# Attention 1: a loop of its own, with split context as weights of the values product and the division on GpSimd

## The reference

```python
def _L1_xattn_ref(x, context, Wq, Wk, Wv, Wo, bo):
    HEADS = 16
    DIM_HEAD = 64
    SCALE = DIM_HEAD ** (-0.5)
    ...
    q = (x @ Wq).reshape(B, N, HEADS, DIM_HEAD).transpose(0, 2, 1, 3)
    k = (context @ Wk).reshape(B, M, HEADS, DIM_HEAD).transpose(0, 2, 1, 3)
    v = (context @ Wv).reshape(B, M, HEADS, DIM_HEAD).transpose(0, 2, 1, 3)
    dots = jnp.einsum('bhnd,bhmd->bhnm', q, k) * SCALE
    attn = jax.nn.softmax(dots, axis=-1)
    out = jnp.einsum('bhnm,bhmd->bhnd', attn, v)
    out = out.transpose(0, 2, 1, 3).reshape(B, N, HEADS * DIM_HEAD)
    return out @ Wo + bo
```

## Time and profile before

| what | us |
|---|---|
| median of 3 executions | 4946.03 |
| the profiled execution | 4941.79 |
| its span | 4940.1 |
| of that, attention 1's rounds, first scores to the next stage's first matmul | 1349.3 to 2873.7 |

### The profile page before, as it was taken

How to read it: one execution, slowest core, us unless ns; L and a number is a source line. 1 busy time by engine, 2 the same in 40 slices (tenths; PEclk the granted TensorE clock), 3 DMA queues, 4 the chain that set the end, 5 groups by cost and what they waited for, 6 DMA issues and landing times. The chain is left out here.

```text
span 4940.1 us, 100893 instructions
## 1 busy us (share of the span) xinstructions
PE 4273.6 (87%) x34007; PEld 3601.8 (73%) x34007; DVE 3320.7 (67%) x6505; ACT 2358.4 (48%) x5328; POOL 1276.1 (26%) x1182
## 2 busy tenths in 40 slices
PE   5399999994599999999999968788699999959684
PEld 4277777773499999999999955566577777747573
DVE  4477777765566666666666677887677777755545
ACT  0056666662144444444444446666366666634341
POOL 0122222221201101111010036676222222214320
PEclk6589999996799999999999988898799999979796
DMA  7344545430100100010010010000445454410371
GB/s 239 104 102 110 110 99 117 104 74 10 43 20 25 30 25 25 20 34 23 22 35 20 11 35 18 18 0 1 90 110 111 100 118 105 103 45 1 86 184 39
DMA packets 102723, 316.97 MB, mean 64 GB/s; under 512 B 36391, under 2 KB 44889, under 8 KB 102425
## 3 DMA queue, kind: packets, MB, share of 16 engines
q1 hardware_dynamic: 98840, 294.71, 25.5%
q10 hardware_dynamic: 3584, 18.43, 1.0%
HBM read 146.07 MB, written 19.54 MB: 34 GB/s over the span
## 5 line engine op out<-in xcount | busy, mean ns | idle before, releaser
L1394 ACT ACTIVATE a1m_prob<-a1m_ps_s,a1m_neg_max 128x500 f32<-128x500 f32 x672 | 447.3, 674 | 585.4 <-DVE a1m_neg_max L1318 585.4
L1237 PE MATMUL a1m_ps_o<-a1m_cn,a1m_prob_t 125*128 125x96 f32 x5376 | 633.2, 274 | 0.4 <-issue 0.4
L1237 PEld LDWEIGHTS a1m_ps_o<-a1m_cn,a1m_prob_t 125*128 125x128 f32 x5376 | 619.8, 192 | 0.6 <-issue 0.6
L1315 DVE TENSOR_REDUCE a1m_bank_max<-a1m_ps_s 128x1 f32<-128x500 f32 x672 | 455.7, 678 | 214.5 <-PE a1m_ps_s L1203 212.6
L729 DVE TENSOR_REDUCE a0m_bank_max<-a0m_ps_s 112x1 f32<-112x500 f32 x768 | 489.0, 669 | 153.4 <-PE a0m_ps_s L593 148.7
L729 DVE TENSOR_REDUCE a2m_bank_max<-a2m_ps_s 112x1 f32<-112x500 f32 x768 | 488.9, 669 | 149.3 <-PE a2m_ps_s L593 144.8
L1203 PE MATMUL a1m_ps_s<-a1m_cxt,a1m_qhi 98*128 98x500 f32 x1344 | 442.9, 411 | 19.8 <-issue 13.1
L812 ACT ACTIVATE a0m_prob_t<-a0m_ring 125x448 f32<-125x448 f32 x768 | 391.3, 545 | 96.7 <-PE a0m_ring L547 92.8
L812 ACT ACTIVATE a2m_prob_t<-a2m_ring 125x448 f32<-125x448 f32 x768 | 391.2, 545 | 94.7 <-PE a2m_ring L547 90.9
L1165 POOL TENSOR_TENSOR a1m_cxt<-a1m_raw,g_zeros 98x1500 fp32r<-98x1500 f32 x32 | 86.6, 2707 | 1281.9 <-PE a1m_ps_s L1203 1234.1
L1219 PE MATMUL a1m_ps_t<-g_ident,a1m_prob 128*125 128x128 f32 x2688 | 377.7, 277 | 0.4 <-ACT a1m_prob_t L1402 0.3
(11 more groups left out here) (778 smaller groups left out, 9251.7 us busy)
## 6 DMA issues: line engine op xcount, KB each, us to landing
a0m_ks<-a0m_k_hi SPq DMA_DIRECT2D x256, 187.5 KB
a2m_ks<-a2m_k_hi SPq DMA_DIRECT2D x256, 187.5 KB
a0m_ks<-a0m_k_lo SPq DMA_DIRECT2D x128, 187.5 KB
a2m_ks<-a2m_k_lo SPq DMA_DIRECT2D x128, 187.5 KB
ctx_t<-cprep_tr ACTq DMA_DIRECT2D x32, 562.5 KB
a0m_raw<-ctx_t SPq DMA_DIRECT2D x32, 562.5 KB
a1m_raw<-ctx_t SPq DMA_DIRECT2D x32, 562.5 KB
a2m_raw<-ctx_t SPq DMA_DIRECT2D x32, 562.5 KB
```

What stands on the lines that cost most here:

```text
L1237: m = pe.matmul(ps_o[at, 0:C], prob_t[:, u % 2, t, at], cn[:, h, t, :], start=(t == 0), stop=(t == KT - 1))
L1315: dve.tensor_reduce(bank_max[:, s, k:k + 1], ps_s[:, k, 0:BK], AX.X, ALU.max).then_inc(bank_maxed, 1)
L1394: act.activation(prob[:, s, k * BK:(k + 1) * BK], ps_s[:, k, 0:BK], ACT.Exp, bias=neg_max[:, s:s + 1], accum_out=bank_den[:, s, k:k + 1]). ...
```

## The change

Attention 1 gets its own function, `attend_heads`; `attention` keeps the case of attention 3. In it:

- The probabilities are divided before they are turned: GpSimd multiplies each bank (128x500) by the reciprocal of the denominator, in place (`divide`). `normalise`, `o_turn` and its copy go.
- The turned probabilities are split into float32r parts: ACT copies the high part of each bank from PSUM (`high_part`), DVE subtracts it from PSUM and writes the low part (`low_part`). Each bank of PSUM for the turned probabilities is used once per unit (three banks, `ps_t`), where there were two in turn.
- The context for the values product is split too, by GpSimd, and is now the weights (96 columns), with the turned probabilities of two or three units as the moving side (256 or 384 columns), in three products of parts for each of the twelve tiles. The result comes out turned.
- The products of a group of units are spread over steps by the table `pieces`; the four queries stand in steps 5, 7 and 10, project in step 3.
- PE's step is scores of u, project or one query, turn of u - 1, sums, a further query. DVE's is maxima of u, low part of u - 2, denominator of u, queries. ACT's is exps of u, the copy of a finished group, high part of u - 1. GpSimd's is the division of u and one piece of the context's split. The clears at the stage's start go, and the queries' bias, which is zero here.
- The three `pick` tables of `constants` go; where they were read (twice each, on ACT), `pick` writes the same from columns of `g.ident`.

```diff
             pool.memset(g.hm64[:], 1.0).then_inc(cleared, 1)
-            picks = ((g.pick_f0, 12, 64), (g.pick_f1, ME, 128), (g.pick_f2, 8, 256))
-            for tile, _, _ in picks:
-                pool.memset(tile[:], 1.0).then_inc(cleared, 1)
...
-            for tile, cols, width in picks:
-                v = tile[:].rearrange("e (c w) -> e c w", w=width)
-                pool.affine_select(out=v, in_=v, compare_op=ALU.is_equal, fill=0.0, base=0,
-                                   pattern=[[-1, cols], [0, width]], channel_multiplier=1).then_inc(cleared, 1)
...
+def attend_heads(nc, g, name, ctx_d, ctx_t, ob, a_w, vo):
...
+    nu, heads, hq, nq, width = 2 * HEADS * L // P, HEADS, TC // PAIR, HEADS // (TC // PAIR), HEADS * L
+    su, total, R = nu // 2, nu * NP, 4
+    members = ((0, 1), (2, 3), (4, 5, 6))
+    place = (0, 1, 2, 3, 0, 1, 2, 3, 2, 0, 1, 2, 3, 1)
+    free_at = (-1, 0, 0, 0, 1, 1, 2, 2, 3, 3, 3, 4, 4, 5)
+    pieces = {4: (0, 0, 0, 0, 6, False), 5: (0, 0, 0, 6, 12, False), 6: (0, 0, 1, 0, 6, False),
+              7: (0, 0, 1, 6, 12, False), 8: (0, 0, 2, 0, 4, True), 9: (0, 0, 2, 4, 12, False),
+              11: (0, 1, 0, 0, 6, False), 12: (0, 1, 0, 6, 12, False), 13: (0, 1, 1, 0, 6, False),
+              0: (-1, 1, 1, 6, 12, False), 1: (-1, 1, 2, 0, 4, True), 2: (-1, 1, 2, 4, 12, False)}
+    ask_at = {5: (0,), 7: (1,), 10: (2, 3)}
...
+        prob = st.sb("prob", [P, 2, S])
+        prob_t = st.sb("prob_t", [NK, 2, KT, R, P], F32R)
...
+        def rounds(eng, step):
+            for u in range(nu):
+                step(0, u, 0)
+            with eng.Fori(0, NP // 2 - 1) as j:
+                for b in range(2):
+                    for u in range(nu):
+                        step(2 * j + b + 1, u, 1 - b)
+            for u in range(nu):
+                step(NP - 1, u, 1)
+            for u in range(4):
+                step(NP, u, 0)
...
+            load_keys(0, 0)
+            load_vals(0)
+            load_keys(1, 1)
+            sp.wait_ge(vals_low, 3)
+            load_vals(1)
+            with sp.Fori(1, NP) as i:
+                for b in range(2):
+                    n = 2 * i + b
+                    sp.wait_ge(scored, BANKS * su * (n - 1))
+                    load_keys(n, b)
+                    sp.wait_ge(vals_low, 3 * n)
+                    load_vals(n)
...
+            def split(whole, high, low, made, done, count):
+                pool.tensor_tensor(high, whole, g.zeros[0:rows, 0:1].broadcast_to([rows, wide]), ALU.add
+                                   ).then_inc(made, 1)
+                pool.wait_ge(made, count)
+                pool.tensor_tensor(low, whole, high.bitcast(F32), ALU.subtract).then_inc(done, 1)
...
+            def divide(i, u):
+                v, s = nu * i + u, u % 2
+                pool.wait_ge(denned, v + 1)
+                for k in range(BANKS):
+                    at = slice(k * BK, (k + 1) * BK)
+                    pool.tensor_tensor(prob[:, s, at], prob[:, s, at], den[:, s:s + 1].broadcast_to([P, BK]), ALU.mult
+                                       ).then_inc(divided, 1)
+            def step(i, u, b):
+                h, s = u // su, u % su
+                if live(i, u, 0):
+                    divide(i, u)
+                n, j, o = 2 * i + h + 1, i + h, 1 - h
+                if s in (2, 3, 4) and among(n, 2 * NP):
+                    split_keys(n, j, o, s - 2)
+                if s in (5, 6) and among(n, 2 * NP):
+                    split_vals(n, o, s - 5)
+                if s == 0 and up(n - 1) and among(n - 1, 2 * NP):
+                    split_vals(n - 1, h, 2)
...
+                    pe.wait_ge(q_kept, nq * (i + 1))
+                rows = slice(u % su * P, (u % su + 1) * P)
+                for k in range(BANKS):
+                    if up(v):
+                        pe.wait_ge(exped, BANKS * (v - 1) + k + 1)
+                    keys = slice(k * BK, (k + 1) * BK)
+                    for n, (part, w) in enumerate(((qhi, 0), (qhi, 1), (qlo, 0))):
+                        m = pe.matmul(ps_s[:, k, 0:BK], part[:, b, h, rows], cxt[:, h, w, keys], start=(n == 0),
+                                      stop=(n == 2))
...
+            def turn(i, u):
+                v = nu * i + u
+                for k in range(BANKS):
+                    pe.wait_ge(divided, BANKS * v + k + 1)
+                    if up(v):
+                        pe.wait_ge(low, BANKS * (v - 1) + k + 1)
+                    for q in range(GT):
+                        t = k * GT + q
+                        m = pe.transpose(ps_t[k][0:NK, q * P:(q + 1) * P], prob[:, u % 2, t * NK:(t + 1) * NK],
+                                         g.ident[:])
+                    m.then_inc(turned, 1)
+            def sums(i, h, x, first, last):
...
+                    if t == first or t % GT == 0:
+                        pe.wait_ge(low, BANKS * end + t // GT + 1)
+                    for q, (w, p) in enumerate(((0, 0), (0, 1), (1, 0))):
+                        m = pe.matmul(out, cn[:, h, w, t * C:(t + 1) * C], prob_t[:, p, t, at:at + len(units), :],
+                                      start=(t == 0 and q == 0), stop=(t == KT - 1 and q == 2))
+                if last == KT:
+                    m.then_inc(summed, 1)
...
+            def step(i, u, b):
+                d, h, x, first, last, behind = pieces.get(u, (0, 0, 0, 0, 0, None))
+                ready = behind is not None and among(i + d, NP)
+                if live(i, u, 0):
+                    scores(i, u, b)
+                if u == 3 and among(i - 1, NP):
+                    project(i - 1)
+                asks = ask_at.get(u, ()) if live(i, u, 0) else ()
+                for q in asks[:1]:
+                    queries(i + 1, q)
+                if live(i, u, 1):
+                    turn(*((i, u - 1) if u > 0 else (i - 1, nu - 1)))
+                if ready and not behind:
+                    sums(i + d, h, x, first, last)
+                for q in asks[1:]:
+                    queries(i + 1, q)
+                if ready and behind:
+                    sums(i + d, h, x, first, last)
...
+            def queries(i, b, q):
+                src = ps_q[0:C, 0:hq * PAIR].rearrange("p (h b l) -> p b h l", h=hq, b=2)
...
+                dve.wait_ge(q_made, n + 1)
+                dve.tensor_copy(hi, src).then_inc(q_high, 1)
+                dve.wait_ge(q_high, n + 1)
+                dve.tensor_tensor(lo, src, hi.bitcast(F32), ALU.subtract).then_inc(q_kept, 1)
...
+            def low_part(i, u):
+                v = nu * i + u
+                for k in range(BANKS):
+                    tiles = slice(k * GT, (k + 1) * GT)
+                    dve.wait_ge(high, BANKS * v + k + 1)
+                    dve.tensor_tensor(prob_t[:, 1, tiles, place[u], :],
+                                      ps_t[k][0:NK, :].rearrange("p (t r) -> p t r", t=GT),
+                                      prob_t[:, 0, tiles, place[u], :].bitcast(F32), ALU.subtract).then_inc(low, 1)
+            def denominator(i, u):
+                v, s = nu * i + u, u % 2
+                dve.wait_ge(exped, BANKS * (v + 1))
+                if up(v - 1):
+                    dve.wait_ge(divided, BANKS * (v - 1))
+                dve.tensor_reduce(den[:, s:s + 1], bank_den[:, s, :], AX.X, ALU.add).then_inc(added, 1)
+                dve.wait_ge(added, v + 1)
+                dve.reciprocal(den[:, s:s + 1], den[:, s:s + 1]).then_inc(denned, 1)
+            def step(i, u, b):
+                if live(i, u, 0):
+                    maxima(i, u)
+                if live(i, u, 2):
+                    low_part(*((i, u - 2) if u > 1 else (i - 1, nu + u - 2)))
+                if live(i, u, 0):
+                    denominator(i, u)
+                    for q in ask_at.get(u, ()):
+                        queries(i + 1, 1 - b, q)
...
+            def high_part(i, u):
+                v = nu * i + u
+                done = 6 * i + free_at[u]
+                if up(done):
+                    act.wait_ge(summed, done)
+                for k in range(BANKS):
+                    act.wait_ge(turned, BANKS * v + k + 1)
+                    act.activation(prob_t[:, 0, k * GT:(k + 1) * GT, place[u], :],
+                                   ps_t[k][0:NK, :].rearrange("p (t r) -> p t r", t=GT), ACT.Copy).then_inc(high, 1)
...
+            def step(i, u, b):
+                if live(i, u, 0):
+                    exps(i, u)
+                d, h, x, _, last, _ = pieces.get(u, (0, 0, 0, 0, 0, None))
+                if last == KT and among(i + d, NP):
+                    keep_sums(i + d, h, x)
+                if u == 3 and among(i - 1, NP):
+                    out(i - 1)
+                if live(i, u, 1):
+                    high_part(*((i, u - 1) if u > 0 else (i - 1, nu - 1)))
...
-        full = heads == HEADS
-        gp = 1 if full else 2
+        if heads == HEADS:
+            attend_heads(nc, g, name, ctx_d, ctx_t, ob, a_w, vo)
+            return
...
```

(68 more changed lines are left out.)

237 lines of the change are left out of this document (177 added, 60 removed).

## The result

The changed kernel takes 5335.5 us (median of 4 runs, 5328.6 to 5348.4) where the kernel before takes 4947.5 (4 runs, 4934.3 to 4950.6): 1.079 times the time, with a 95% interval of 1.076 to 1.081. The forecast was 5346 us. Against the execution on which the sum was made, 4941.8, the profiled one of after (5331.3) has +389.5; forecast +404.

The account below looks back on a forecast made before the run. Attention 1 was taken as bound by PE's list. Profiled 4941.8 us, +302 for the added wait, +125 for the clock, -16 for the stage's start, -6.6 for the tables gave 5346 us, range 5200 to 5510.

Parts of the forecast that it names:

- The added wait: Attention 1: PE's turn waits for DVE's low part behind the maxima; rounds 111.7 us against 92.9, +302 us in all.
- The clock: Attention 1: PE's new 1.6 us gaps, in ten steps of fourteen, let the clock fall; 7.8 us a round, +125 us.
- half of them: Share of a round's ten PE gaps assumed to lose 1.56 us each to low clock: 5 x 1.56 = 7.8 us.
- rival 1: PE's gaps in attention 1 cost no clock: rounds of 111.7 us, 5221 us in all; chance 0.18.
- The products: Values product on PE: 0.123 us per 256 columns, 0.178 per 384; 30.5 us a round against 37.1.
- What is covered: Attention 1: work of ACT, GpSimd and SP's loads fits within the longer steps; GpSimd 5.5 to 6.5 us, under 7.7.
- that meeting: DVE subtraction while GpSimd runs, once seen at 3.64 us instead of 0.62; costed at nothing in the new loop.
- The rest: Outside the rounds: clears at the stage's start gone, -16 us; tables gone, -6.6 us; fill and drain 0.
- rival 2: Every gap in attention 1 drops the clock, a slow spell reaching the next gap: 5711 us; chance 0.11.
- Rival 3: PE does not stand in attention 1, if banks were freed before the maxima: rounds of 85.7, 4804 us; chance 0.07.
- Rival 4: GpSimd's division or split slower than any row, over 7.7 us a step: 112 us on top; chance 0.04.

Follow-up runs that it names:

- e1: The changed kernel with fourteen spare transposes on PE before the turn, in the ten steps with a gap and neither project nor query: 5203.7 us.
- e2: The changed kernel with five spare transposes on PE before the turn, in the ten steps with a gap and neither project nor query: 5210.4 us.
- e5: The changed kernel with two spare transposes on PE before the turn, in the ten steps with a gap and neither project nor query: 5240.9 us.
- e3: The changed kernel with only PE's order altered, the products of a finished group standing between scores and turn: 4959.4 us.
- e7: The changed kernel with products before the turn and the queries moved from steps 5, 7, 10, 10 to 1, 8, 10, 12: 4870.2 us, 0.985 times the kernel before.
- e6: The changed kernel with a spare fourth 128x500 operation on GpSimd before each unit's division: 5349.9 us.
- e8: The changed kernel with products before the turn, queries moved to steps 1, 8, 10, 12, and a spare 128x500 GpSimd operation before each division: 4870.2 us.
- e4: The changed kernel with only DVE's order altered, the low part of u - 2 before the maxima of u: 5097.8 us.

## Why the prediction was right, point by point

- **The added wait** was the core, and it holds in place, size and number: in most steps the turn starts 3.84 to 3.86 after the first score (3.87 forecast), and ordinary steps take 7.66 (7.7). e1 isolates the round without spells: 111.2 against 111.7. Step 3 was costed a little high, 6.84 (7.1). Step 10 takes 7.8 (8.2), but its last 0.4, the late second copy that holds the next maxima back, is there: it falls in step 11, whose turn starts at 4.24 and which takes 8.05.
- **The clock**: 1.56 us a spell, five a round, 7.8 a round. The spell's length was taken from one gap in the earlier trace rows, of three that cost 3.06, 1.56 and nothing, and "half of them" lay between bounds and was a choice, not a reading: that both hit to a tenth is luck. e1, e2 and e5 show that the spells hang on PE's idle time; why one gap of 1.65 us has one and the next has not stays open. The rule under "HAM oscillation — how this bites in real kernels" in the Trainium skill (TensorE: Matmul & The Clock Gate) would have left these gaps free of cost, and with it rival 1 would hold; the trace contradicts it with half of the gaps of 1.65 us.
- **The products**: from the first start to the next instruction, 18 products of 256 columns take 2.19 us in the rows at 3234.03 and 2.12 in e3's at 2616.22, so 0.118 to 0.122 each (0.123), and 24 of 384 take 4.19 in e7, so 0.175 (0.178). That is 11 to 15 ns above the columns at 2.4 GHz, where I took 17: a round's products take 29.6 to 30.2 us, forecast 30.5. By the 2.5 ns of the Trainium skill (the same page, "Wait — 56ns, not 53.3ns?") the estimate would be 27.4; the rows here lie nearer to the forecast, so leaving that rule out of the sum was right. The prediction called both rows evidence against it. Only the first is: 0.21 us for two products. The second row's 0.39 us is a length and not a distance between starts.
- **What is covered**: DVE and GpSimd are busy 53% and 54% of a stretch, a little under the 60% expected. The division took 1.02 us a bank (1.1), the split of 500 columns 1.02 and 1.25 (2.2 for both), and e6 adds another microsecond a step for nothing. The low part is 0.68 each (0.69), with GpSimd busy over half of the time, so costing that meeting at nothing was right. At steps of 6.3 us on average (88.2 / 14) the slack is nearly used up: the microsecond of e8 costs some 0.4 us a round. So the sentence "if steps were shorter, GpSimd would be the cover that fails" was a little too gloomy for PE's order; e4 shows when it does fail, when the maxima come late.
- **The rest**: start -17.3 (-16), tables -6.8 (-6.6). Some 5 us more came from untouched stages ahead of attention 1, for which no step of the prediction stands.
- **The rivals**: rival 1 is refuted by the clock of 0.92 and by e1; rival 2 by the spells' number. Rival 3 was out at once, since the order is as read; what it says of the way out is half right. With the low part before the maxima (e4) the round is 104.0 us and not 85.7, because the maxima then wait for ACT, and the division comes late. What comes near 85.7 is e7, where the banks are freed no earlier but asked for later. Its profiled execution takes 4865 us where the rival's sum says 4804. Of the 61 between, the waits left are some 40 (16 x 2.5) and the six loop ends, 2.1 dearer each than before, 13. Rival 4's price was not met: 1.02 us a bank.

## What to carry to other kernels

When an engine's list is reordered, ask for each instruction which buffer it overwrites and where on the other engine's list the reader of that buffer stands: here some 372 us hung on the order of two lines on PE, and the same exchange on DVE gave some 234 and moved the wait to another pair of engines. The added wait on PE cost twice here, 25.5 us a round for its length and 7.8 for the clock behind it, so price both, and put work that is ready (here the products) into the gap. The busy shares of PE and DVE fell together here, and two waits that pointed at each other were the cause, not a slow instruction.

## What was not expected of the hardware

Two gaps of the same 1.65 us, a step apart, had different effects on the clock (the rows at 3232.41 and 3240.06), so a gap's length alone doesn't decide. And yet the length counts sharply: two spare transposes, which cut the gap only from 1.65 to 1.43 us, took away all but three of the spells behind such gaps. e5 is some 90 us faster than after, of the 128 that e1 gains with fourteen, and its PE still waits 208.5 us for the low part from 1500 to 2900. What it keeps is mostly behind step 11's gap of 1.73 us and the ends of the hardware loop.
